# Mixer pass 1 of a macaron block: another order of chunk sums and rstd, and idle products around the first transposes

## The reference, cut to what matters

```python
x = x + 0.5 * ffn(layernorm(x), Wg, W11, W12, W2)      # 8 experts, top 2 of them per token
x = x + attn(layernorm(x), ...)
x = x + 0.5 * ffn(layernorm(x), Wg, W11, W12, W2)

# attn(T):
rms = sqrt(mean(T * T, -1) + 1e-6)
xz = (T / rms * norm_scale) @ in_w.T + in_b
x, z = split(xz, 2, -1);  gate = sigmoid(z)
xc = pointwise(depthwise_conv(x, 3 taps) + dw_b) + pw_b
y = ssm_forward(xc) + ssm_backward(xc)                 # 64 states each, along the sequence
return T + (y * gate) @ out_w.T + out_b
```

## Time and profile before

| | us |
|---|---|
| median of the runs | 987.4 |
| the profiled execution | 985.32 |
| its span in the trace | 983.5 |
| TensorE busy, over the span | 903.3 (92%) |
| GpSimd busy | 575.8 (59%) |
| VectorE busy | 582.7 (59%) |

### The profile page before, as it was taken

How to read it: one execution, slowest core, us unless ns; L and a number is a source line. 1 busy time by engine, 2 the same in 40 slices (tenths; PEclk the granted TensorE clock), 3 DMA queues, 4 the chain that set the end, 5 groups by cost and what they waited for, 6 DMA issues and landing times.

```text
span 983.5 us, 19046 instructions
## 1 busy us (share of the span) xinstructions
PE 903.3 (92%) x5396; PEld 778.3 (79%) x5399; DVE 582.7 (59%) x1394; ACT 391.2 (40%) x768; POOL 575.8 (59%) x605
## 2 busy tenths in 40 slices
PE   7769999999999999949897996899999999999994
PEld 6658888888888888827775874688888888888883
DVE  3986565675665655556726887555555555555551
ACT  3644244343443433325443775133333333333331
POOL 3435565666666665357514651577777777777762
PEclk9979999999999999968999996899999999999997
DMA  9654525526336281086202555654433333333332
GB/s 313 204 179 138 205 69 189 185 75 205 131 126 203 94 267 56 28 267 193 65 1 85 162 179 176 214 139 77 78 55 75 54 74 75 53 75 53 54 46 25
DMA packets 83936, 121.50 MB, mean 124 GB/s; under 512 B 12944, under 2 KB 62736, under 8 KB 83888
## 3 DMA queue, kind: packets, MB, share of 16 engines
q1 hardware_dynamic: 45376, 57.88, 18.1%
q0 software_dynamic: 24992, 37.32, 17.5%
q10 hardware_dynamic: 13520, 25.70, 7.7%
HBM read 73.62 MB, written 47.25 MB: 123 GB/s over the span
## 4 chain that ended last, share of the span: by engine, by line
PE 76%; DVE 7%; DMA 5%; ACT 5%; POOL 3%; issue 3%; ACTq 1%; SPq 0%; POOLq 0%
PE bank L1456 40%; PE bank L1479 20%; PE bank L1465 6%; PE bank L1448 3%; PE bank L1577 3%; ACT work L879 1%; DMA seq<-xt 1%; PE bank L1635 1%; DMA seq<-x_rows 1%; PE bank L1625 1%; ACT work L812 1%; ACT work L870 1%; DMA out_rows<-yb,idx_i 1%; PE bank L1394 1%; DMA seq<-y_rows 1%
## 5 line engine op out<-in xcount | busy, mean ns | idle before, releaser
L1165 DVE TENSOR_TENSOR sg<-sg,bank 128x512 f32<-128x512 f32 x142 | 97.7, 688 | 282.7 <-ACT sg L741 282.7
L1456 PE MATMUL bank<-w_hi,xt_hi 128*128 x568 | 237.8, 419 | 4.5 <-DVE xt_lo L1154 4.4
L1456 PE MATMUL bank<-w_hi,xt_lo 128*128 x568 | 225.1, 396 | 0.0
L1456 PE MATMUL bank<-w_lo,xt_hi 128*128 x568 | 225.0, 396 | 0.0
L733 ACT ACTIVATE yb<-bank,gates_in 128x256 f32<-128x256 f32 x142 | 67.3, 474 | 313.8 <-PE bank L1479 276.0
L551 POOL DMA_INDIRECT xg<-xn_rows,idx_i x142 | 140.1, 987 | 72.6 <-issue 41.4
L555 POOL DMA_INDIRECT gates_in<-gate_rows,idx_g x142 | 136.2, 959 | 48.0 <-issue 42.7
L1479 PE MATMUL bank<-w_hi,ft_hi 128*128 x568 | 160.3, 282 | 2.2 <-ACT yb L733 2.2
L1479 PE MATMUL bank<-w_lo,ft_hi 128*128 x568 | 160.5, 283 | 0.0
L1479 PE MATMUL bank<-w_hi,ft_lo 128*128 x568 | 160.4, 282 | 0.0
L565 POOL DMA_INDIRECT out_rows<-yb,idx_i x71 | 114.9, 1619 | 63.2 <-ACT yb L733 53.4
(11 more groups left out here) (289 smaller groups left out, 1293.8 us busy)
## 6 DMA issues: line engine op xcount, KB each, us to landing
w_lo<-w_lo_rows SPq DMA_DIRECT2D x32, 512.0 KB, 4.6
w_lo_rows<-w_lo ACTq DMA_DIRECT2D x16, 512.0 KB
xn_rows<-work SPq DMA_DIRECT2D x14, 512.0 KB, 3.4
seq<-y_rows SPq DMA_DIRECT2D x10, 512.0 KB, 5.2
x_all<-x SPq DMA_DIRECT2D x8, 512.0 KB, 9.0
w_lo_rows<-in_sb ACTq DMA_DIRECT2D x16, 256.0 KB, 2.4
gate<-x SPq DMA_DIRECT2D x16, 256.0 KB, 5.8
seq<-w ACTq DMA_DIRECT2D x7, 512.0 KB, 4.5
```

The costliest lines, as they stand in the source:

```text
L1165: nc.vector.tensor_tensor(sg[p], sg[p], ps_g[p][:], ALU.mult).then_inc(f_step, 1)
L1456: last = nc.tensor.matmul(dst[p][:], xt[p][:, c, :], of(w), start=(c == 0 and n == 0), stop=(c == DC - 1 and n == len(parts) - 1))
```

## The change

Three edits:

- GpSimd runs rsqrt_rms(i) ahead of sum_choices(i + 1), and no longer adds chunk 1. Its list becomes rstd 0, rstd 1, sum 2, rstd 2, sum 3, and so on to rstd 6, sum 7, rstd 7.
- VectorE adds the two rows of chunk 1 itself, as it does for chunk 0. The counts of half_sum move by one.
- TensorE waits for chunk 0's moments (mv_ready) behind its twelve idle products and runs three more, then the transposes of chunk 0, eight more idle products, and the transposes of chunk 1.

```diff
             for i in range(NCH):
-                if i + 1 < NCH:
+                rsqrt_rms(i, i % 2)
+                if 2 <= i + 1 < NCH:
                     sum_choices(i + 1)
-                rsqrt_rms(i, i % 2)
@@ stats_x1
-                if i == 0:
-                    dve.wait_ge(y_in[0], 32)
+                if i < 2:
+                    dve.wait_ge(y_in[y_buffer[i]], 32)
                     link(nc.vector.tensor_tensor(y_rows[0], y_rows[0], y_rows[1], ALU.add))
                 else:
-                    dve.wait_ge(half_sum, i)
+                    dve.wait_ge(half_sum, i - 1)
@@ tensor
             keep_busy(ps_t1[1][0][:], before.unsqueeze(1).to_broadcast([P, G, P]), 12)
+            pe.wait_ge(mv_ready, 1)
+            keep_busy(ps_t1[1][0][:], before.unsqueeze(1).to_broadcast([P, G, P]), 3)
             transposes_1(0, 0)
+            keep_busy(ps_t1[1][0][:], before.unsqueeze(1).to_broadcast([P, G, P]), 8)
             transposes_1(1, 1)
```

## The result

The changed kernel takes 990.73 us (median of 10 runs, 988.57 to 993.31) against 986.93 for the one before (10 runs). The ratio is 1.0041, 95% interval 1.0029 to 1.0054: slower by 4.0 us, with 2.9 to 5.3 in the interval (the medians alone differ by 3.8). The forecast was 990.3, +2.95 us. The profiled execution of the changed kernel took 991.96 us (span 989.8), 1.2 above its median.

The account below looks back on a forecast made before the run. TensorE was 92% busy, but around the change the chain ran through GpSimd to ScalarE. Chunk 7's addition 4.0 us late, less ScalarE's 1.1 slack, gave +2.95 on 987.4: 990.3 us, range 987.2 to 992.1; products counted 0.

Parts of the forecast that it names:

- The ring: GpSimd and VectorE: each chunk's sum waits behind the last chunk's rstd, a loop of 9.77 us, 8.9 without the scan.
- Before there was no such ring.: Old GpSimd order: chunk i+1 was added ahead of chunk i's rstd, so VectorE found each sum ready.
- Chunk 0's early start is worth 0.1 us: GpSimd's first rstd: two VectorE additions stall L518 and L519, so L525 ends at 435.3 against 435.39.
- after 435: Sign that the forecast is right: chunk 0's L525 on GpSimd ends later than 435; 433.3 would show it wrong.
- L518's 0.87 us: GpSimd's L518: its extra time per turn is waiting for the VectorE scan started just behind the moments.
- rival c: L518's extra 0.87 us is waking an idle GpSimd, so chunks 2 and 3 pay too: +4.7 us, 992.1; chance 0.08.
- The copies' stalls move out of the way: VectorE's two-element copies, one taking 1.85 us beside GpSimd's sum, mostly escape such stalls; worth nothing.
- The idle products cost 0 to 0.2 us and their effects are hidden: TensorE's eleven products: benefit up to 0.9 us per transpose group, covered by the wait for chunk 2's rstd; taken as 0.
- Rival d: TensorE's idle products do not hold the clock, transposes stay at 1.96 us; same time as forecast, within its 0.68.
- Rival a: VectorE and GpSimd stalls do not bite and the ring is short enough: -1.6 us, 985.8; chance 0.12.
- rival b: The ring is there but its scan stall goes, the start gaining nothing: 0 us, 987.4; chance 0.12.

Follow-up runs that it names:

- e1: Changed kernel with GpSimd again adding a chunk before it needs to (sum 2 ahead of rstd 1); ratio to the kernel before 0.9997.
- e2: Kernel before with only GpSimd's order changed, no addition moved to VectorE and no added idle products; ratio to the kernel before 1.0045.
- f2: f1 with VectorE waiting for chunk 0's rstd before it adds chunk 1; ratio to the kernel before 0.9997.
- g2: f3 with VectorE's wait before adding chunk 1 ended earlier, at GpSimd's L519 and L520 of chunk 0; ratio to the kernel before 0.9959.
- e4: Changed kernel with VectorE's forward scans of chunks 0 to 3 moved behind the last chunk's moments; ratio to the kernel before 1.0021.
- g3: Changed kernel without its three and eight idle products; ratio to the kernel before 1.0027.
- e3: Kernel before with only the change's three and eight idle products added on TensorE; ratio to the kernel before 1.0014.
- f1: e1 without the three and the eight idle products; ratio to the kernel before 0.9999.
- f3: f2 with VectorE's scans 0 to 4 moved behind the low part of chunk 6; ratio to the kernel before 0.9989.
- g1: f3 plus the eleven idle products, six more behind gate_in(0), and VectorE's wait ended at GpSimd's L519 and L520; ratio to the kernel before 0.9972.

## Why the prediction was right, point by point

*The ring.* This was the forecast, and it held: e1 removes it and e2 adds it alone. The additions were forecast at 442.6, 451.5, 460.4, 470.2, 479.9 and 489.7, and came at 442.27, 451.25, 460.29, 470.12, 479.90 and 489.80. The stage began 0.3 us earlier, so relative to it the last is 0.4 us late: turns of 9.83, 9.78 and 9.90 us for the 9.77 of the rows. Chunk 7's rstd came at 495.77 (forecast 495.7), its transposes at 497.93 (497.8). The stage's +3.38 us has the same 0.4 over the +2.95. The total of 990.3 looks closer to 990.73 than the working was: its base, 987.4, was 0.5 above the 986.93 of more runs, and the shift was some 1 us short of the ratio's 4.0. That these two offset each other is luck.

*"Before there was no such ring."* Not so for chunks 5 and 6. There chunk 5's addition stood behind a copy that was held until sum 6 ended (466.05 to 468.42), and sum 6 stood behind chunk 4's rstd, which waited for chunk 4's moments. That is a loop of 9.88 us, as long as the new one. What the change did is to be read at its two ends: chunk 4's addition, which a sum had held up by only 0.3 us before, is 1.9 us later behind the first L1230 (33.6 against 31.7), and in the last turn, where no sum was left to hold a copy, 7.48 us became 9.90, so that chunk 7's is 4.4 us later. The turns between cost nothing new. The forecast is unharmed because it took chunk 7's old place from its row, 485.70, and not from a count of turns.

*Chunk 0's early start is worth 0.1 us.* Right, 0.2 measured, and for the stated reason: f2 takes the two additions away and rstd 0 moves from 8.24 to 6.39. L525 ended at 434.93, just short of the sign "after 435", as the stage had begun 0.3 us earlier. By the rule of the Trainium skill ("SBUF — State Buffer", Who interferes with whom) this is what should happen. For L518 and L519 the trace agrees: 1.07 and 1.22 us beside additions of 1.19 and 1.22, and 0.20 and 0.24 in f2. For L522 it does not: in g2 neither it nor the addition beside it waited.

*L518's 0.87 us is VectorE's scan, not waking (rival c).* Right. The row of 445.44 has 0.19 us after 3.30 us of idleness, and e4 shows it in the later turns as well. At chunk 5 the scan came 0.14 us later behind the moments than at chunk 4 (473.27, and L518 at 473.30 took 0.19) and stalled L519 instead (1.01 us): the price is nearly the same.

*The copies' stalls move out of the way.* Wrong. They stayed, 2.36 us at 467.66 and 2.33 at 477.47, and for chunks 5 and 6 they, and not an idle VectorE, stand between the sum and the addition. They cost nothing extra, since the addition has to wait for that same sum.

*The idle products cost 0 to 0.2 us and their effects are hidden.* The zero in the sum held for chunk 7, as g3 shows. The working did not: it looked for the cost at the transposes, and it came one step later. ssm_in(0)'s first six products took 2.91 us for 1.64, after 3.44 us of idleness in front of chunk 2's transposes. Here the ring covers that from chunk 4 on; without one, e3's profile has a stage 1.8 us longer, 1.5 of it in ssm_in(0). The three products ahead of the first transposes did not keep them warm in the changed kernel's profile (1.97 us); in e1 and e4, which have them too, they were warm (1.09), and so they were in e2 and g3, which have not. Rival d, cold transposes at no cost, so came true for the first group of transposes and not for the second (1.10 us).

*Rival a, faster, and rival b, no change.* Both needed GpSimd's stalls to go, and in the changed kernel they did not. Where experiments made them go, the gain did not always follow: e4, with the ring in place, gives back 1.4 us of the stage, which is less than rival b's 3 us, as chunk 7's stall came back; f2, without the ring, gained nothing on f1; f3 and g2, with the scans' stalls gone too, are 1.9 and 2.6 us shorter than the kernel before. Rival a itself, both kinds of stall gone in the changed order, no run tried.

## What to carry to other kernels

When a producer is put behind a consumer of the previous item on an in-order engine, write down the loop it closes and add it up from the trace: here 1.2 us of addition, 1.9 of moments, 4.2 of rstd with its stall and 2.4 of sum exceed the 8.45 us of TensorE's shortest turn. What it costs is the difference to the turns that stood there before, so read those first: here two of them were as long already, and the loss came from the others. An engine that is 59% busy can still set the pace that way. Idle products that warm work off the path can move the idle time to where the path is, and the clock may fall there: of the four profiles with just the eleven products more, three show it (2.91, 2.61 and 2.33 us for ssm_in(0)'s first six in the changed kernel, e3 and e4, against 1.64) and e1's does not. That it makes the whole kernel slower is not shown: e3's interval includes no change.

## What the runs showed of the hardware

- One GpSimd operation and a VectorE addition did not hold each other: in g2 L522, a power of four elements per partition, had been under way for 0.15 us when the addition began, and took 1.05 us, the addition its 1.23 (1.04 and 1.23 in g1). L518, L519 and in e3 L525, which came while an addition ran, waited for it (1.07, 1.22 and 1.07 us for 0.2). Which operation stands beside the addition decides whether it costs anything.
- Two VectorE scans back to back held two small GpSimd operations and let one through between them: L518 took 1.06, L519 0.23 and L520 1.12 us in e4.
- A copy of two elements per partition on VectorE was held by a GpSimd sum until the sum's end: 1.85 to 2.36 us instead of some 0.16, in the kernel before and the changed one.
- TensorE's clock at the first transposes differed between profiles of kernels that are the same up to that point: 1.97 us for eight in the changed kernel after 2.48 us of idleness, 1.09 in e4 after 2.97, with fifteen products ahead of them in both. A forecast for a short warm stretch has to carry both.
